# Node stage of a graph attention and mixture-of-experts layer: transposes between the halves of the products, and the bias added by an accumulating DMA

## The chip, the cores and the metric

The kernel runs on one core of a Trainium2 chip. The metric is the device time of one execution in microseconds. The kernel before took 2589.26 us in the median of 3 runs (2583.23 to 2590.76). A change within about 0.3% cannot be told from none.

## The reference

The layer is a graph attention step over 3125 nodes and 50,000 edges, followed by a mixture of eight experts. Cut to what the change touches:

```python
x = x + relu(gat(layernorm(x)) + bias)      # gat: softmax-weighted sum over the edges of each node and its own row
xn = layernorm(x)                           # eps 1e-5
proj = xn @ Wp.T                            # only its length is needed
gate = (proj / |proj|) @ l2norm(sim).T / temperature       # 8 scores per node, top 2
x = x + experts(xn)                         # needs xn of every node
```

The kernel never forms `proj`. With the Gram matrix G = Wp.T Wp (built earlier, held as two fp16 parts, upper triangle doubled) the squared length is xn . (G xn), and the scores come from xn times a premultiplied 1024x8 matrix `Msim`.

## The kernel before

The program is a row of blocks of code, each with one instruction list per engine, written by hand: the order in each list is the order of execution, and semaphores with counted waits order the engines. No planner takes part. The stages are projection, edge tables, softmax maxima, edge gathering with products, the node stage, slot assignment and the experts.

The change is in the node stage (L1043 to L1230). It handles the 3125 nodes in 25 blocks of 125 rows; every tile is 125 partitions by 1024 columns, and `p = i % 2` picks one of two buffers. For block i:

- SP loads two tiles of 500 KB: `own` (the node's own projected row) and `xt` (the input row), L1078 and L1079. It waits until `x2` of block i-2 is done.
- ACT scales `own` by the weight of the self loop, four instructions on L1187 (`scale_own`). It waits for both loads.
- DVE runs `layer_out`: four instructions on L1128 (gathered sum times 1/z plus `own`), the bias add on L1130, and ReLU plus `xt` on L1131, which ends block i's `x2`. `moments` (L1137 to L1140) gives mean and variance.
- ACT takes the root (L1194); DVE finishes the reciprocal in five tiny instructions (`inverse_std`, L1146 to L1150); ACT writes the normed rows twice, as fp32 `xn` (L1200) and as the fp16 high part (L1201); DVE's `low` (L1155) writes the fp16 low part.
- PE transposes both parts, 16 instructions (`turn_parts`, L1738); ACT copies them from PSUM to SBUF (`take_turned`, L1207).
- PE multiplies: first half of the triangle (12 matmuls, L1729), the scores (24 small matmuls, L1720), second half (24 matmuls, L1729). DVE's `length_and_scores` (L1160, L1162) reads the result.
- POOL stores `x2` to `out` (L1086) and the two fp16 parts to `x2n_d` (L1088), 500 KB each.

DVE's order in turn i is `inverse_std(i)`, `layer_out(i+1)`, `low(i)`, `moments(i+1)`, `length_and_scores(i-1)`. ACT's is `normed(i)`, `scale_own(i+2)`, `take_turned(i)`. PE's is transposes of block i, first half, scores, second half. POOL's is store of `x2` of block i, then store of the parts of block i. The bias is loaded once, broadcast to 125 partitions (L1073), and DVE waits for it on L1117.

Of the kernel before, what the change touches and what calls it, by code (L numbers as in the profile page):

```python
# [42 lines left out]
ROWS = 125  # L43
# [110 lines left out]
def program(nc, x, src, dst, W, att_src, att_dst, bias, Wp, sim, temp, W1, b1, W2, b2, out):  # L154
# [25 lines left out]
    with ctx:  # L180
# [43 lines left out]
        simT = sbuf(load_ctx, "simT", [P, 2, KD, NX], F16)  # L224
        s_st16, s_stw = sem("ed_st16"), sem("ed_stw")
        s_row = [sem(f"ed_row{p}") for p in range(2)]
        s_out = [sem(f"pj_out{p}") for p in range(2)]
        LATE = BLOCKS - 3
        with ExitStack() as c:
# [54 lines left out]
            with nc.Block() as block:  # L284
                @block.sync
                def _(sp):
                    def load(i):
                        if i >= 2:
                            sp.wait_ge(s_xf, i - 1)
                        sp.dma_start(xt[:, i % 2, :], rows_of(x, i)).then_inc(s_x[i % 2], 16)  # L290
                    load(0)
                    for n in range(4):
                        sp.dma_start(W_f[:, 2 * n:2 * n + 2, :],
                                     W[2 * n * P:(2 * n + 2) * P, :].rearrange("(k p) n -> p k n", p=P)).then_inc(s_ldw[n], 16)
                    load(1)
                    for n, a in enumerate((att_src, att_dst)):
                        sp.dma_start(att_b[:, n, :], a.rearrange("h c -> (h c)").partition_broadcast(ROWS)).then_inc(s_att, 16)
                    for i in range(2, BLOCKS):
                        load(i)
                        if i == 3:  # L300
                            sp.wait_ge(s_wlo, KD)
                            sp.dma_start(Wp_f[:, 1:KD + 1, :], Wp.rearrange("(k p) d -> p k d", p=P)).then_inc(s_ldp, 16)
                        if i == 15:

                            sp.wait_ge(s_rowv, 1)
                            sp.dma_start(lo_d.rearrange("(p r) n -> p (r n)", r=4), rowV[:, 0, :]).then_inc(s_vstore, 16)
                            sp.dma_start(dloc_d.rearrange("(p r) n -> p (r n)", r=4), rowV[:, 1, :]).then_inc(s_vstore, 16)
                    sp.wait_ge(s_vstore, 32)
                    sp.wait_ge(s_tr_ix, 3)
                    for t, d, n in ((stage_lo, lo_d, P), (stage_dl, dloc_d, ROWS)):  # L310
                        sp.dma_start(t, d[0:CHUNK, :].partition_broadcast(n)).then_inc(s_row[0], 16)
                    st_rows = st_d.rearrange("(b r) h -> r b h", r=ROWS)
                    for n, bs in enumerate((slice(0, LATE), slice(LATE, BLOCKS))):
                        sp.wait_ge(s_st16, 2 * n + 2)
                        sp.dma_start(st_rows[:, bs, :], st16[:, bs, :]).then_inc(s_stw, 16)

# [299 lines left out]
        with ExitStack() as c:  # L616
# [11 lines left out]
            w_ps, m_ps = v_all[:, 0:FIRST, :], v_all[:, 3, 0:KD * NX].rearrange("p (k e) -> p k e", e=NX)  # L628
            s_tab, s_zero = sem("ed_tab"), sem("ed_zero")
            s_gr, s_ghi, s_glo, s_m = sem("gr_mm"), sem("gr_hi"), sem("gr_lo"), sem("gr_msim")  # L630
# [28 lines left out]
            with nc.Block() as block:  # L659
                @block.sync  # L660
                def _(sp):
# [6 lines left out]
                    def tables():  # L668

                        sp.wait_ge(s_stw, 32)  # L670
                        sp.wait_ge(s_zero, 1)
# [72 lines left out]
                def _(pe):  # L744
# [3 lines left out]
                    for n in range(FIRST):  # L748
                        gram_piece(pe, n, w_ps[:, n, :])
                    pe.wait_ge(s_tab, 32)  # L750

# [291 lines left out]
        with edge_ctx, acc_ctx:  # L1043
            with ExitStack() as c:
                xt = sbuf(c, "n_xt", [ROWS, 2, D])
                own = sbuf(c, "n_own", [ROWS, 2, D])
                x2 = sbuf(c, "n_x2", [ROWS, 2, D])
                xn = sbuf(c, "n_xn", [ROWS, 2, D])
                bias_b = sbuf(c, "n_bias", [ROWS, D])
# [11 lines left out]
                sc_ps = psum(c, "n_sc", [P, 2, 512])  # L1061
                s_b, s_ch, s_d, s_e = sem("nd_bias"), sem("nd_chain"), sem("nd_d"), sem("nd_e")
                s_x = [sem(f"nd_x{p}") for p in range(2)]
                s_own, s_x2c, s_x2, s_ln, s_var, s_std = sem("nd_own"), sem("nd_x2c"), sem("nd_x2"), sem("nd_ln"), sem("nd_var"), sem("nd_std")
                s_rstd, s_xh = sem("nd_rstd"), sem("nd_xh")
# [4 lines left out]
                with nc.Block() as block:  # L1070
                    @block.sync
                    def _(sp):
                        sp.dma_start(bias_b[:, :], bias.partition_broadcast(ROWS)).then_inc(s_b, 16)  # L1073
                        for i in range(BLOCKS):
# [6 lines left out]
                    @block.gpsimd  # L1081
                    def _(pool):
                        for i in range(BLOCKS):
                            p = i % 2
                            pool.wait_ge(s_x2, i + 1)
                            pool.dma_start(rows_of(out, i), x2[:, p, :]).then_inc(s_out[p], 16)  # L1086
                            pool.wait_ge(s_xn, i + 1)
                            pool.dma_start(rows_of(x2n_d, i), xs[:, p, :, :].rearrange("r n d -> r (n d)")).then_inc(s_xo[p], 16)  # L1088
                        for p in range(2):
                            pool.wait_ge(s_out[p], 16 * ((BLOCKS + 1 - p) // 2))  # L1090
                            pool.wait_ge(s_xo[p], 16 * ((BLOCKS + 1 - p) // 2))

                    @block.vector
                    def _(dve):
# [21 lines left out]
                        dve.tensor_tensor(w_own, wk[:, 0, :, :], z_inv, ALU.mult).then_inc(s_d, 1)  # L1116
                        dve.wait_ge(s_b, 16)  # L1117

                        def layer_out(i):

                            p = i % 2
                            near = Chain(dve, s_x2c, 2 * i)
                            dve.wait_ge(s_own, i + 1)
                            if i >= 2:
                                dve.wait_ge(s_out[p], 16 * (i // 2))
                            for h in range(HEADS):
                                sl = slice(h * C, (h + 1) * C)
                                ins = dve.scalar_tensor_tensor(x2[:, p, sl], acc[:, i, sl], z_inv[:, i, h:h + 1], own[:, p, sl], ALU.mult, ALU.add)  # L1128
                            near(ins)
                            near(dve.tensor_tensor(own[:, p, :], x2[:, p, :], bias_b[:, :], ALU.add))  # L1130
                            dve.scalar_tensor_tensor(x2[:, p, :], own[:, p, :], 0.0, xt[:, p, :], ALU.max, ALU.add).then_inc(s_x2, 1)  # L1131
# [20 lines left out]
                        def low(i):  # L1152
                            p = i % 2
                            dve.wait_ge(s_xh, i + 1)
                            dve.tensor_tensor(xs[:, p, 1, :], xn[:, p, :], xs[:, p, 0, :], ALU.subtract).then_inc(s_xn, 1)  # L1155

                        def length_and_scores(i):
                            p = i % 2
                            dve.wait_ge(s_mm, i + 1)
                            dve.scalar_tensor_tensor(pj_ps[0:ROWS, p, :], pj_ps[0:ROWS, p, :], 1.0 / WS, xn[:, p, :], ALU.mult, ALU.mult,  # L1160
                                                     accum_out=nsq[:, i:i + 1])
# [4 lines left out]
                        for i in range(BLOCKS):  # L1166
# [4 lines left out]
                            if i + 1 < BLOCKS:  # L1171
                                moments(i + 1)
                            if i >= 1:
                                length_and_scores(i - 1)
                        length_and_scores(BLOCKS - 1)

                    @block.scalar
                    def _(act):
# [4 lines left out]
                        def scale_own(i):  # L1183
                            p = i % 2
                            act.wait_ge(s_x[p], 32 * (i // 2 + 1))
                            for h in range(HEADS):
# [3 lines left out]
                        def normed(i):  # L1190
# [3 lines left out]
                            act.activation(ln[:, p, 3:4], ln[:, p, 2:3], ACT.Sqrt).then_inc(s_std, 1)  # L1194
                            act.wait_ge(s_rstd, i + 1)
                            if i >= 2:
                                act.wait_ge(s_sc, i - 1)
                                act.wait_ge(s_tr, i - 1)
                                act.wait_ge(s_xo[p], 16 * (i // 2))
                            act.activation(xn[:, p, :], x2[:, p, :], ACT.Identity, bias=ln[:, p, 8:9], scale=ln[:, p, 7:8])  # L1200
                            act.activation(xs[:, p, 0, :], x2[:, p, :], ACT.Identity, bias=ln[:, p, 8:9], scale=ln[:, p, 7:8]).then_inc(s_xh, 1)  # L1201
# [15 lines left out]
                    def _(pe):  # L1217
                        for i in range(BLOCKS):
                            p = i % 2
                            pe.wait_ge(s_xn, i + 1)  # L1220
                            if i >= 1:
                                pe.wait_ge(s_xnT, i)
                            turn_parts(pe, tr_ps, xs[:, p, :, :], ident16).then_inc(s_tr, 1)
                            pe.wait_ge(s_xnT, i + 1)
# [3 lines left out]
                            triangle(pe, pj_ps[0:ROWS, p, :], lhs, gram, 0, range(KD // 2))  # L1228
                            product(pe, sc_ps[0:ROWS, p, 0:NX], lhs, Msim[:, :, :, :], range(KD), KD)
                            triangle(pe, pj_ps[0:ROWS, p, :], lhs, gram, 1, range(KD)).then_inc(s_mm, 1)  # L1230

# [555 lines left out]
```

## Time and profile before

| | |
|---|---|
| profiled execution, own time | 2587.55 us |
| its span in the trace | 2585.8 us |
| runs | median 2589.26 us, 2583.23 to 2590.76 |
| busy over the span | PE 80%, DVE 59%, ACT 43%, POOL 28% |
| granted TensorE clock, mean over the span | 0.892 |
| node stage in the trace | about 1456 to 1794 us |

The trace lists the instructions of each engine with start, duration and what ended the idle time before them. SPq and POOL rows of DMA instructions are the time of issue, not of the transfer; the landing is given apart. PEclk 1.00 is 2.4 GHz and 0.50 is 1.2 GHz. A DMA share of 1.00 would be all 16 DMA engines busy.

### The profile page before, as it was taken

Reading aid. Unit: us, or ns where it says so; the run is one execution under the profiler, and the core shown is the slowest. Engines: PE = TensorE matmul, PEld = TensorE weight load, DVE = VectorE, ACT = ScalarE, POOL = GpSimd, SP = SyncE. Lnnn points to the kernel's source line nnn. Section 1 sums busy time; section 2 is a strip of 40 time slices with the busy share of each in tenths; the row PEclk is TensorE's granted clock in tenths of the full one; section 3 lists DMA queues with packets and bytes.
Section 4 is the critical chain, followed back from the end, with each engine's and each line's share of the span. In section 5 each row is a group of like instructions: output and inputs, shape, how many; then the busy total and the mean of one; then the engine's idle time right before and its main releaser. Section 6 shows DMA issues by size and latency. Waiting matters only on the chain. (4 is left out here: it accounts for less than half of the span.)

```text
span 2585.8 us, 53583 instructions
## 1 busy us (share of the span) xinstructions
PE 2069.9 (80%) x14842; PEld 1476.4 (57%) x14843; DVE 1520.5 (59%) x4456; ACT 1117.3 (43%) x2399; POOL 716.5 (28%) x933
## 2 busy tenths in 40 slices
PE   2888987666678888888888478786498999898997
PEld 1555554444378788887888466664244444454553
DVE  3776764777766666666666576875744334434333
ACT  2333441111156676766667454542344334434332
POOL 0001000000055555555555200000223233333332
PEclk9899997555799999999999787988699999999999
DMA  4433343331078988988898544444545555564542
GB/s 137 154 110 113 118 150 94 122 133 59 1 252 299 310 300 297 309 299 296 289 305 299 183 173 168 172 162 148 205 138 198 207 176 200 199 213 159 174 159 89
DMA packets 141057, 489.14 MB, mean 189 GB/s; under 512 B 22449, under 2 KB 22659, under 8 KB 138829
## 3 DMA queue, kind: packets, MB, share of 16 engines
q0 software_dynamic: 98912, 346.99, 40.3%
q1 hardware_dynamic: 41853, 140.70, 14.9%
q8 instruction: 48, 0.79, 0.1%
q10 hardware_dynamic: 216, 0.43, 0.0%
q14 instruction: 28, 0.23, 0.0%
HBM read 418.06 MB, written 81.27 MB: 193 GB/s over the span
## 5 line engine op out<-in xcount | busy, mean ns | idle before, releaser
L1018 PE MATMUL main_ps<-rows,O 128*125 128x256 f16 x4992 | 614.0, 281 | 117.3 <-DVE acc L959 52.9
L1018 PEld LDWEIGHTS main_ps<-rows,O 128*125 128x125 f16 x4992 | 553.4, 141 | 139.0 <-issue 76.0
L1004 ACT ACTIVATE O<-O,pk 128x125 f16<-128x125 f16 x1664 | 499.5, 388 | 231.0 <-DVE O L974 196.8
L945 POOL DMA_INDIRECT rows<-projected,idx x416 | 396.1, 952 | 306.5 <-PE small_ps L1023 190.7
L978 DVE TENSOR_SCALAR O<-O,pk 128x125 f16<-128x125 f16 x1664 | 320.7, 278 | 14.8
L1720 PE MATMUL pj_ps<-gram,xsT 128*125 128x512 f16 x1200 | 291.8, 403 | 45.8 <-ACT xsT L382 44.6
L1671 PE MATMUL x_h<-w_p,gram 128*128 x1344 | 309.7, 388 | 13.8 <-ACT gram L1624 8.8
L1686 PE MATMUL x_o<-w_p,gram 128*128 x1344 | 312.5, 383 | 1.4 <-ACT gram L1640 1.4
L1720 PEld LDWEIGHTS pj_ps<-gram,xsT 128*125 128x125 f16 x1200 | 169.9, 145 | 155.9 <-ACT xsT L382 52.8
L1729 PE MATMUL n_pj<-gram,PK 128*125 128x512 f16 (+3 forms) x900 | 184.6, 367 | 55.5 <-ACT PK L1207 55.5
L1671 PEld LDWEIGHTS x_h<-w_p,gram 128*128 128x128 f16 x1344 | 132.2, 100 | 168.2 <-issue 29.4
L1686 PEld LDWEIGHTS x_o<-w_p,gram 128*128 128x128 f16 x1344 | 130.6, 99 | 150.3 <-issue 7.2
L974 DVE TENSOR_SCALAR O<-iota,pk 128x125 f16<-128x125 f16 x416 | 113.9, 274 | 142.7 <-PE small_ps L1023 101.3
L1729 PEld LDWEIGHTS n_pj<-gram,PK 128*125 128x125 f16 x900 | 126.6, 155 | 111.5 <-ACT PK L1207 59.9
L1632 ACT ACTIVATE h_g<-h_b 128x512 f32<-128x512 f32 x56 | 35.3, 630 | 290.0 <-DVE h_b L1604 290.0
L1594 DVE SCALAR_TENSOR_TENSOR x_o<-x_o,b_t 128x1024 f32<-128x1024 f32 x56 | 68.9, 1231 | 146.7 <-PE x_o L1686 146.7
L1570 POOL DMA_INDIRECT out_dram<-x_y,xi x56 | 76.6, 1367 | 235.4 <-DVE x_y L1597 235.4
L1624 ACT ACTIVATE gram<-x_tr 128x2048 f16<-128x2048 f16 x56 | 104.9, 1873 | 83.7 <-PE x_tr L1738 83.7
L1597 DVE SCALAR_TENSOR_TENSOR x_y<-x_o,gate_of_slot,x_y 128x1024 f32<-128x1024 f32 x56 | 71.9, 1283 | 100.6 <-DMA x_y<-out_dram,xi 98.7
L940 POOL COPY idx<-srcT 128x4 int32 (+1 forms) x104 | 20.5, 197 | 314.7 <-SPq L932 314.2
L740 ACT ACTIVATE d_p<-d_ps 128x64 f32 (+1 forms) x104 | 23.2, 223 | 188.2 <-PE d_ps L767 188.2
L1604 DVE SCALAR_TENSOR_TENSOR h_b<-x_h,b_b 128x512 f32<-128x512 f32 x56 | 38.6, 690 | 111.3 <-PE x_h L1671 102.3
(325 smaller groups left out, 2622.4 us busy)
## 6 DMA issues: line engine op xcount, KB each, us to landing
w_f<-in_L_ffn_W_dram SPq DMA_DIRECT2D x14, 2048.0 KB
b_t<-in_L_ffn_b_dram SPq DMA_DIRECT2D x56, 512.0 KB
xt<-in_x_dram SPq DMA_DIRECT2D x25, 500.0 KB
projected_f<-xp_f POOLq DMA_DIRECT2D x25, 500.0 KB, 3.7
projected<-xp POOLq DMA_DIRECT2D x25, 500.0 KB, 4.8
n_own<-projected_f SPq DMA_DIRECT2D x25, 500.0 KB
n_xt<-in_x_dram SPq DMA_DIRECT2D x25, 500.0 KB
out_dram<-n_x POOLq DMA_DIRECT2D x25, 500.0 KB, 9.9
```

The lines of the kernel that those rows point to most:

```text
L945: pool.indirect_dma_start(out=rows[:, 4 * p + k, :, :].rearrange("k n d -> k (n d)"), out_offset=None, in_=xp_d[:, :], in_offset=bass.Indi ...
L974: dve.tensor_scalar(O[:, k, 0, 0:ROWS], iota16[:, 0:ROWS], pk[:, p, k, 0:1], None, ALU.is_equal).then_inc(s_oh, 1)
L978: ins = dve.tensor_scalar(O[:, k, 1 + h, 0:ROWS], O[:, k, 0, 0:ROWS], pk[:, p, k, 1 + h:2 + h], None, ALU.mult)
L1004: ins = act.activation(O[:, k, 1 + HEADS + h, 0:ROWS], O[:, k, 0, 0:ROWS], ACT.Copy, scale=pk[:, p, k, w:w + 1])
L1018: pe.matmul(main_ps[0:ROWS, h * C:(h + 1) * C], O[:, k, 1 + HEADS * a + h, 0:ROWS], rows[:, 4 * p + k, b, h * C:(h + 1) * C], start=first ...
L1570: pool.indirect_dma_start(out=out[:, :], out_offset=bass.IndirectOffsetOnAxis(ap=xi[:, 2 + p, :], axis=0), in_=y[:, p, :], in_offset=None, ...
L1597: dve.scalar_tensor_tensor(y[:, p, :], o_ps[:, p, :], at1(gateT, i), y[:, p, :], ALU.mult, ALU.add).then_inc(s_eo, 1)
L1624: act.activation(xgT[:, p, :, :, :], tr_ps[:, :, :, :], ACT.Copy).then_inc(s_xT, 1)
L1671: ins = pe.matmul(h_ps[:, :], xgT[:, p, a, k, :], w, start=(k == 0 and a == b), stop=(k == KD - 1 and a == 1))
L1686: ins = pe.matmul(o_ps[:, p, n * 512:(n + 1) * 512], hT[:, p, a, f, :], w, start=(f == 0 and a == b), stop=(f == KF - 1 and a == 1))
L1720: ins = pe.matmul(out, lhs[:, a, k, :], rhs[:, b, k, :], start=(k == 0 and a == b), stop=(k == last - 1 and a == 1))
L1729: ins = pe.matmul(out[:, cols], lhs[:, a, k, :], rhs[:, b, k, cols], start=(k == 0 and a == b), stop=True, skip_group_check=True)
```

## The change

Four edits in the node stage, and a merging of semaphores elsewhere.

1. The 16 transposes of block i+1 are issued between the scores and the second half of block i. Only block 0's stand ahead of the loop.
2. `xn` gets a third buffer; `length_and_scores(i-2)` instead of (i-1) stands at the end of DVE's turn i, and ACT's wait for it is one block looser.
3. The bias add leaves DVE. After `scale_own(i)`, POOL issues a DMA from `bias_b` to `own` in SBUF that adds (`add_bias`). The first two stand ahead of POOL's loop, the one for block i+2 after the two stores of its turn i. DVE's `layer_out` waits for that DMA, and writes the sum to `own` instead of `x2`.
4. The wait for the bias load moves from DVE to the first `scale_own`.
5. `s_stw` and `s_tab` of the edge tables become one semaphore, with the wait raised from 32 to 64.

```diff
-                xn = sbuf(c, "n_xn", [ROWS, 2, D])
+                xn = sbuf(c, "n_xn", [ROWS, 3, D])
...
+                        def add_bias(i):
+
+                            p = i % 2
+                            pool.wait_ge(s_own, i + 1)
+                            pool.dma_start(own[:, p, :], bias_b[:, :], accum_op=ALU.add).then_inc(s_ob[p], 16)
+                        add_bias(0)
+                        add_bias(1)
                         for i in range(BLOCKS):
                             p = i % 2
                             pool.wait_ge(s_x2, i + 1)
                             pool.dma_start(rows_of(out, i), x2[:, p, :]).then_inc(s_out[p], 16)
                             pool.wait_ge(s_xn, i + 1)
                             pool.dma_start(rows_of(x2n_d, i), xs[:, p, :, :].rearrange("r n d -> r (n d)")).then_inc(s_xo[p], 16)
+                            if i + 2 < BLOCKS:
+                                add_bias(i + 2)
...
-                        dve.wait_ge(s_b, 16)
...
-                            near = Chain(dve, s_x2c, 2 * i)
-                            dve.wait_ge(s_own, i + 1)
+                            dve.wait_ge(s_ob[p], 16 * (i // 2 + 1))
...
-                                ins = dve.scalar_tensor_tensor(x2[:, p, sl], acc[:, i, sl], z_inv[:, i, h:h + 1], own[:, p, sl], ALU.mult, ALU.add)
-                            near(ins)
-                            near(dve.tensor_tensor(own[:, p, :], x2[:, p, :], bias_b[:, :], ALU.add))
+                                ins = dve.scalar_tensor_tensor(own[:, p, sl], acc[:, i, sl], z_inv[:, i, h:h + 1], own[:, p, sl], ALU.mult, ALU.add)
+                            ins.then_inc(s_x2c, 1)
+                            dve.wait_ge(s_x2c, i + 1)
...
-                            if i >= 1:
-                                length_and_scores(i - 1)
-                        length_and_scores(BLOCKS - 1)
+                            if i >= 2:
+                                length_and_scores(i - 2)
+                        for i in (BLOCKS - 2, BLOCKS - 1):
+                            length_and_scores(i)
...
-                            act.wait_ge(s_x[p], 32 * (i // 2 + 1))
+                            act.wait_ge(s_x[p], 32 * (i // 2 + 1) + (16 if p == 0 else 0))
...
+                            if i >= 3:
+                                act.wait_ge(s_sc, i - 2)
                             if i >= 2:
-                                act.wait_ge(s_sc, i - 1)
...
-                        for i in range(BLOCKS):
-                            p = i % 2
+                        def turn(i):
                             pe.wait_ge(s_xn, i + 1)
                             if i >= 1:
                                 pe.wait_ge(s_xnT, i)
-                            turn_parts(pe, tr_ps, xs[:, p, :, :], ident16).then_inc(s_tr, 1)
+                            turn_parts(pe, tr_ps, xs[:, i % 2, :, :], ident16).then_inc(s_tr, 1)
+                        turn(0)
+                        for i in range(BLOCKS):
+                            p = i % 2
                             pe.wait_ge(s_xnT, i + 1)
...
                             product(pe, sc_ps[0:ROWS, p, 0:NX], lhs, Msim[:, :, :, :], range(KD), KD)
+                            if i + 1 < BLOCKS:
+                                turn(i + 1)
                             triangle(pe, pj_ps[0:ROWS, p, :], lhs, gram, 1, range(KD)).then_inc(s_mm, 1)
```

## Rows read from the trace of the kernel before

**Rows 1.** Span; timeline at both ends of the stage (start us, us, engine).

```profile
span 2585.8 us, 53583 instructions
...
1476.51 0.25 SPq L1078 DMA_DIRECT2D n_own<-projected_f  x1
...
1482.56 1.67 DVE L1128 SCALAR_TENSOR_TENSOR n_x<-acc,n_wk,n_own 125x256 f32<-125x256 f32 x4
...
1486.77 0.25 SPq L1078 DMA_DIRECT2D n_own<-projected_f  x1
...
1768.53 1.22 DVE L1131 SCALAR_TENSOR_TENSOR n_x<-n_own,n_xt 125x1024 f32<-125x1024 f32 x1
...
1794.12 0.26 SPq L1330 DMA_DIRECT2D tcol<-n_L_ffn_temperature_dram  x1
```

**Rows 2.** Timeline, one block at full clock; in brackets idle time before and its releaser.

```profile
1625.06 1.04 PE L1738 MATMUL n_tr<-ident,PK 125*128 125x125 f16 x16
1626.14 1.84 ACT L1207 ACTIVATE PK<-n_tr 128x2000 f16<-128x2000 f16 x1 [1.97 <-PE n_tr L1738]
1628.03 1.85 PE L1729 MATMUL n_pj<-gram,PK 128*125 128x512 f16 x12 [1.93 <-ACT PK L1207]
1629.12 1.66 DVE L1128 SCALAR_TENSOR_TENSOR n_x<-acc,n_wk,n_own 125x256 f32<-125x256 f32 x4
...
1630.82 1.22 DVE L1130 TENSOR_TENSOR n_own<-n_x,n_bias 125x1024 f32<-125x1024 f32 x1
1631.08 4.42 PE L1729 MATMUL n_pj<-gram,PK 128*125 128x512 f16 x24
1632.07 1.23 DVE L1131 SCALAR_TENSOR_TENSOR n_x<-n_own,n_xt 125x1024 f32<-125x1024 f32 x1
...
1635.33 1.04 PE L1738 MATMUL n_tr<-ident,PK 125*128 125x125 f16 x16
```

**Rows 3.** Timeline, from the end of a block's x2 to its loads, stores and next scaling.

```profile
1608.27 1.22 DVE L1131 SCALAR_TENSOR_TENSOR n_x<-n_own,n_xt 125x1024 f32<-125x1024 f32 x1
1609.52 0.25 SPq L1078 DMA_DIRECT2D n_own<-projected_f  x1
1610.92 0.52 POOL L1088 DMA_DIRECT2D x_after_gnn_normed<-PK  x1 [12.49 <-DVE PK L1155]
1611.44 0.52 POOL L1086 DMA_DIRECT2D out_dram<-n_x  x1
1622.47 1.71 ACT L1187 ACTIVATE n_own<-n_own,n_wk 125x256 f32<-125x256 f32 x4 [1.13 <-DMA n_xt<-in_x_dram]
```

**Rows 4.** Waits between the second and the last block: total us, times, longest.

```profile
ACT n_own L1187 <- DMA n_xt<-in_x_dram: 66.8, 21, 4.5
PE n_pj L1729 <- ACT PK L1207: 51.7, 23, 3.3
```

**Rows 5.** Timeline, the first two scalings, each released by its loads.

```profile
1470.46 1.70 ACT L1187 ACTIVATE n_own<-n_own,n_wk 125x256 f32<-125x256 f32 x4 [10.08 <-DMA n_xt<-in_x_dram]
1478.29 1.70 ACT L1187 ACTIVATE n_own<-n_own,n_wk 125x256 f32<-125x256 f32 x4 [6.12 <-DMA n_xt<-in_x_dram]
```

**Rows 6.** Windows: us, busy us of five engines, clock, DMA share, GB/s.

```profile
1465.00:1475.00 10.00, 0.00 (x0) 0.00 (x0) 2.67 (x5) 1.70 (x4) 0.00 (x0) 0.50 0.32 131
1612.00:1616.00 4.00, 3.83 (x33) 2.83 (x32) 1.23 (x3) 0.13 (x1) 0.00 (x0) 0.95 0.90 286
1616.00:1620.00 4.00, 2.24 (x23) 1.93 (x23) 2.33 (x11) 2.83 (x3) 0.00 (x0) 1.00 0.33 135
```

**Rows 7.** Issue to landing: stores of x2 (all; the first), stores of parts (all).

```profile
DMA to landing us min/median/max: 5.0/9.9/10.5
...
DMA to landing us min/median/max: 7.8/7.8/7.8
...
DMA to landing us min/median/max: 3.6/7.7/8.2
```

**Rows 8.** Window of a stretch at half clock, columns as above.

```profile
1605.50:1612.40 6.90, 6.90 (x40) 5.33 (x39) 6.62 (x11) 4.01 (x6) 1.04 (x2) 0.51 0.28 92
```

More of the change, by code:

```diff
@@ L224, in program @@
         simT = sbuf(load_ctx, "simT", [P, 2, KD, NX], F16)
-        s_st16, s_stw = sem("ed_st16"), sem("ed_stw")
+        s_st16, s_tab = sem("ed_st16"), sem("ed_tab")
         s_row = [sem(f"ed_row{p}") for p in range(2)]
@@ L314, in _ @@
                         sp.wait_ge(s_st16, 2 * n + 2)
-                        sp.dma_start(st_rows[:, bs, :], st16[:, bs, :]).then_inc(s_stw, 16)
+                        sp.dma_start(st_rows[:, bs, :], st16[:, bs, :]).then_inc(s_tab, 16)
                 @block.gpsimd
@@ L628, in program @@
             w_ps, m_ps = v_all[:, 0:FIRST, :], v_all[:, 3, 0:KD * NX].rearrange("p (k e) -> p k e", e=NX)
-            s_tab, s_zero = sem("ed_tab"), sem("ed_zero")
+            s_zero = sem("ed_zero")
             s_gr, s_ghi, s_glo, s_m = sem("gr_mm"), sem("gr_hi"), sem("gr_lo"), sem("gr_msim")
@@ L668, in tables @@
                     def tables():
-                        sp.wait_ge(s_stw, 32)
+                        sp.wait_ge(s_tab, 32)
                         sp.wait_ge(s_zero, 1)
@@ L749, in _ @@
                         gram_piece(pe, n, w_ps[:, n, :])
-                    pe.wait_ge(s_tab, 32)
+                    pe.wait_ge(s_tab, 64)
                     def body(i, j, p):
@@ L1061, in program @@
                 sc_ps = psum(c, "n_sc", [P, 2, 512])
-                s_b, s_ch, s_d, s_e = sem("nd_bias"), sem("nd_chain"), sem("nd_d"), sem("nd_e")
+                s_ch, s_d, s_e = sem("nd_chain"), sem("nd_d"), sem("nd_e")
                 s_x = [sem(f"nd_x{p}") for p in range(2)]
+                s_ob = [sem(f"nd_own_bias{p}") for p in range(2)]
                 s_own, s_x2c, s_x2, s_ln, s_var, s_std = sem("nd_own"), sem("nd_x2c"), sem("nd_x2"), sem("nd_ln"), sem("nd_var"), sem("nd_std")
@@ L1072, in _ @@
                     def _(sp):
-                        sp.dma_start(bias_b[:, :], bias.partition_broadcast(ROWS)).then_inc(s_b, 16)
+                        sp.dma_start(bias_b[:, :], bias.partition_broadcast(ROWS)).then_inc(s_x[0], 16)
                         for i in range(BLOCKS):
@@ L1154, in low @@
                             dve.wait_ge(s_xh, i + 1)
-                            dve.tensor_tensor(xs[:, p, 1, :], xn[:, p, :], xs[:, p, 0, :], ALU.subtract).then_inc(s_xn, 1)
+                            dve.tensor_tensor(xs[:, p, 1, :], xn[:, i % 3, :], xs[:, p, 0, :], ALU.subtract).then_inc(s_xn, 1)
                         def length_and_scores(i):
@@ L1159, in length_and_scores @@
                             dve.wait_ge(s_mm, i + 1)
-                            dve.scalar_tensor_tensor(pj_ps[0:ROWS, p, :], pj_ps[0:ROWS, p, :], 1.0 / WS, xn[:, p, :], ALU.mult, ALU.mult,
+                            dve.scalar_tensor_tensor(pj_ps[0:ROWS, p, :], pj_ps[0:ROWS, p, :], 1.0 / WS, xn[:, i % 3, :], ALU.mult, ALU.mult,
                                                      accum_out=nsq[:, i:i + 1])
@@ L1195, in normed @@
                             act.wait_ge(s_rstd, i + 1)
+                            if i >= 3:
+                                act.wait_ge(s_sc, i - 2)
                             if i >= 2:
-                                act.wait_ge(s_sc, i - 1)
                                 act.wait_ge(s_tr, i - 1)
                                 act.wait_ge(s_xo[p], 16 * (i // 2))
-                            act.activation(xn[:, p, :], x2[:, p, :], ACT.Identity, bias=ln[:, p, 8:9], scale=ln[:, p, 7:8])
+                            act.activation(xn[:, i % 3, :], x2[:, p, :], ACT.Identity, bias=ln[:, p, 8:9], scale=ln[:, p, 7:8])
                             act.activation(xs[:, p, 0, :], x2[:, p, :], ACT.Identity, bias=ln[:, p, 8:9], scale=ln[:, p, 7:8]).then_inc(s_xh, 1)
```

## The prediction

> **What bounds the kernel now.** I read four views, in this order. The page's slices and the timeline first place the stage. Call X(i) the end of L1131 for block i, when `x2` of that block is done. SP issues the loads for block i+2 0.03 us later, so X(0) is 1476.48, X(1) is 1486.74, X(24) is 1769.75, and the next stage starts at 1794.1 [rows 1]. The mean period is (1769.75 - 1486.74)/23 = 12.30 us per block.
>
> The timeline of one block at 2.4 GHz gives the PE loop. Transposes start at 1625.06, the first half waits for ACT's copy and starts at 1628.03, and the next transposes start at 1635.33 [rows 2]. That is 10.27 us, of which 1.93 is the wait for the copy. The waits view has it 23 times, 51.7 us [rows 4]. Other blocks are longer because the clock is 1.2 GHz for part of them, with PE then busy without a gap [rows 8].
>
> The same view shows a second limit, nearly as close. ACT waits for the loads in 21 blocks of 23, 66.8 us [rows 4]. A load issued at 1609.52 releases the scaling at 1622.47, 12.95 us later [rows 3]. The 23 such pairs run from 12.6 to 14.2. The windows say why. With only SP's loads in flight the DMA share is 0.32, that is 0.32 x 16 = 5.1 engines, at 131 GB/s [rows 6]. The next pair of tiles takes 1478.29 - 1470.46 = 7.83 us [rows 5], so 25 rows of 4 KB per tile and engine at 0.157 us each. The Trainium skill ("DMA: Bandwidth & Descriptors", "Why a DMA increments its semaphore by 16 and not by 1") says that a transfer of this path uses the largest number of engines up to 16 that divides its slowest dimension, 5 for 125 rows, the lowest-numbered ones; the 5.1 agrees.
>
 A pair of loads and two stores keep them busy 7.83 + 2.5 = 10.3 us per block, as long as PE's own loop. The stores land late for it: those of the parts 7.7 us after issue in the median, those of `x2`, issued right behind, 9.9 us [rows 7].
>
> **The change, part by part.** *Transposes between the halves.* ACT's copy now has the second half (4.25 us, 1631.08 to 1635.33) to hide under [rows 2]. PE's loop falls from 10.27 to 1625.06-1626.10 plus 1628.03-1635.33 = 1.04 + 7.30 = 8.3 us at full clock. It pays only where nothing else is later.
>
> *Looser scores and the third `xn`.* No instruction is added. `length_and_scores(i-2)` comes after the second half of i-2, which now ends a block earlier relative to it, so I price its wait at 0. If that cover went, DVE would wait for at most one second half, 4.42 us, and the forecast below has more slack than that.
>
> *Bias add off DVE.* L1130 to L1131 starts is 1.25 us, so `layer_out` shrinks from 4.18 (1629.12 to 1633.30) to 2.93 us [rows 2].
>
> *The adding DMA.* This is the new price. The place decides it. In POOL's list the add for block i+2 stands behind the store of the parts of block i, which waits for `low(i)`, which DVE runs after `layer_out(i+1)`. So it cannot be issued before X(i+1). And `layer_out(i+2)` is the next long piece on DVE and waits for its landing. That closes a loop inside one period:
>
> X(i+1) to the issue of the parts is 1610.92 - 1609.49 = 1.43; the second DMA of the pair is issued 0.52 later, at 1.95 [rows 3]. The add takes the place that the store of `x2` has now. Its landing time, A, is in no row. Nearest is that store, same size, same queue, same neighbours: 9.9 us. Below, the same two stores with no load beside them land after 5.0, and a lone one after 3.6 [rows 7]; above, an add that moves twice the rows costs 8 more of them, each alternating with one of a load, 16 x 0.157 = 2.5 us, giving 12.4. I take 9.9, since X(i+1) also issues the next loads 1.4 us ahead, as now. Then 0.1 us to wake DVE (estimate) and 2.93: period = 1.95 + 9.9 + 0.1 + 2.93 = 14.9 us.
>
> A second loop runs over two periods. Loads slow from 12.95 to 12.95 + 1.25 = 14.2 us by the add's own rows, then scaling 1.71, POOL's start 0.3 (estimate from 0.29 between the end of `low` and the issue), A, 0.1, 2.93: (19.2 + A)/2 = 14.6 us. Less, but close. The five engines need 7.83 + 3 x 1.25 = 11.6. PE needs 8.3, and at most twice that, 16.7, in a block wholly at 1.2 GHz.
>
> *What is queued behind the wait.* While POOL waits for the scaling of block i+2, the store of `x2(i+1)` waits behind it. It is needed two periods later and costs 0. Behind DVE's wait stands everything: `low`, so the transposes, so PE's second half. That is in the period.
>
> *Prologue.* Scaling 0 ends at 1472.16 [rows 5]. The add follows at 1472.46 and lands after 7.8, the time of the first store beside loads [rows 7]; `layer_out(0)` ends at 1472.46 + 7.8 + 0.1 + 2.93 = 1483.3. DVE's second `layer_out` started 6.08 after X(0) [rows 1]; kept so, X(1) = 1483.3 + 6.1 + 2.9 = 1492.3, later by 5.5 us.
>
> *Tail.* After X(24), with the durations of [rows 2]: transposes of 23 from 1.3 (1.22 for `low`) to 2.3, second half of 22 to 6.6, first half and scores of 23 (1631.08 - 1628.03 = 3.05) to 9.7, transposes of 24 to 10.7, second half of 23 to 15.0, first half and scores of 24 to 18.0, its second half to 22.4, then 1.8 to the next stage: 24.2 us, against 1794.12 - 1769.75 = 24.4 now [rows 1]. That is -0.2.
>
> *Bias wait and merged semaphores.* The bias is ahead of the first loads in SP's queue, and the scaling waits for those anyway: 0. The table loads follow the table stores through SP's own wait, so 64 is reached when 32 was: 0.
>
> Sum: 5.5 + 23 x (14.9 - 12.3) - 0.2 = 5.5 + 59.8 - 0.2 = +65.1 us. The profiled execution took 2587.55 us, 1.7 below the median of the runs, so 2587.55 + 65.1 = 2652.7, in round numbers 2653 us. Every microsecond of A is worth 23 us.
>
> **Rivals.** *The add reads twice.* The add has to fetch both `own` and `bias_b`. If that doubles its rows, A = 12.4, period 17.4, 23 x 5.1 + 5.3 = +122: 2710 us. Nothing in the trace shows an adding DMA. The Trainium skill ("Collectives: The Full Stack", "The bandwidth ceiling: the fold count and why AG ≠ RS ≠ AR") says that an add in the DMA path needs two source reads, and that this halved a reduce-scatter's rate; no row here bears on it.
>
> *PE stays at 1.2 GHz.* With some 6 us of idle time per period, a slower PE would need 16.7 us: 23 x 4.4 + 5.3 = +107, 2694 us. For it: while PE idled before its first block the clock was 0.50 [rows 6]. Against: it is back at 0.95 to 1.00 a few microseconds after a stretch at 0.51, although PE waits in each block [rows 6, 8].
>
> *Less contention.* The add is SBUF to SBUF and may be on fewer or other engines than the loads. With A = 7.7, like the first store of a pair, and loads at 12.95: (18.0 + 7.7)/2 = 12.9, so 23 x 0.6 + 5 = +19: 2606 us. The DMA page of the Trainium skill, in the section named above, lets GpSimd's queue place a 125-row transfer either on 16 engines or on 5 consecutive ones that rotate; the second would give something like this.
>
> *The landing is as without loads.* A = 5.0: the one-period loop is 10.0, the other (19.2 + 5.0)/2 = 12.1. 23 x (-0.2) + 2.7 = -2: 2586 us, no change. The gain of PE is then hidden by the loads.
>
> *Faster.* The add runs wholly off the five engines of the loads and lands as the fastest store, A = 3.6: (18.0 + 3.6)/2 = 10.8, still above the 10.3 of those engines. 23 x (-1.5) + 1.3 = -33: 2554 us. It decides from A below about 5.3, where (19.2 + A)/2 passes 12.3. For it speaks that once the stores' first burst is over two thirds of the engines are idle, 1 - 0.33 [rows 6]. Against it speak the medians of 7.7 and 9.9 us of the stores that POOL issues now [rows 7].
>
> **How the numbers follow.** The forecast with A from 9.3 to 10.5 has 0.48. The double read has 0.13, the slow clock 0.07, less contention 0.15; these are all slower, 0.83. No change has 0.11 and faster 0.06. 0.3% is 7.8 us, which is also what a measurement can tell. The range from 2592 to 2712 us takes in all slower cases and leaves out no change and faster, 0.17, and a little above; the likeliest case by itself is 2639 to 2667.
>
> **What would show it.** Period 14.9 us between L1078 issues; DVE idle ahead of L1128, some 5 us per block, released by the add's landing near 9.9 us; PE idle ahead of the transposes, released by L1155; no wait of L1729 for L1207; five-engine share of DMA with longer loads, about 14 us. Wrong if DVE's wait for the add is below 1 us, if L1128 is released by ACT, or if the stage (1456 to 1794) becomes shorter than 338 us.

## The result and the profile after

The changed kernel takes 2692.88 us in the median (2690.13 to 2694.91, 4 runs) against 2586.24 for the kernel before (2579.61 to 2590.76, 4 runs). The ratio is 1.042, 95% interval 1.0396 to 1.0444: slower. That lies in the range given. The forecast was 2653, so the loss is 107 us where 65 were forecast.

Line numbers shift in the changed kernel: `scale_own` is L1196, the adding DMA L1088, `layer_out` L1136 and L1139, `low` L1163, the copy of the transposes L1217, the transposes L1752. First the ends of the stage in its timeline, which answer to [rows 1]:

```profile
span 2691.7 us, 53581 instructions
...
1460.59 0.26 SPq L1074 DMA_DIRECT2D n_bias<-in_L_gnn_bias_dram  x1
...
1488.36 0.25 SPq L1079 DMA_DIRECT2D n_own<-projected_f  x1
...
1498.26 0.25 SPq L1079 DMA_DIRECT2D n_own<-projected_f  x1
...
1874.70 1.22 DVE L1139 SCALAR_TENSOR_TENSOR n_x<-n_own,n_xt 125x1024 f32<-125x1024 f32 x1
...
1901.89 0.26 SPq L1344 DMA_DIRECT2D tcol<-n_L_ffn_temperature_dram  x1
```

The stage, from the load of the bias to the first load of the next stage, takes 1901.89 - 1460.59 = 441.3 us. Before it took 337.9, since the same load of the bias stood at 1456.20 and the next stage began at 1794.12 [rows 1]. So 103.4 of the 105.9 us between the two spans are in this stage; below, the length of the stage is always taken in this way. X(i) is, as in the prediction, the end of `layer_out` for block i. From X(1) = 1498.23 to X(24) = 1875.92 it is 377.7 us, 16.4 per block against 12.3.

One period in the timeline, which answers to [rows 2] and [rows 3]:

```profile
1618.24 1.22 DVE L1163 TENSOR_TENSOR PK<-n_xn,PK 125x1024 f16<-125x1024 f32 x1
1618.35 0.25 SPq L1079 DMA_DIRECT2D n_own<-projected_f  x1
...
1619.51 1.86 PE L1752 MATMUL n_tr<-ident,PK 125*128 125x125 f16 x16 [6.95 <-DVE PK L1163]
1619.75 0.53 POOL L1096 DMA_DIRECT2D x_after_gnn_normed<-PK  x1 [14.64 <-DVE PK L1163]
...
1620.27 0.89 POOL L1088 DMA_DIRECT2D n_own<-n_bias  x1
...
1620.82 0.88 POOL L1094 DMA_DIRECT2D out_dram<-n_x  x1
...
1631.68 1.67 DVE L1136 SCALAR_TENSOR_TENSOR n_own<-acc,n_wk,n_own 125x256 f32<-125x256 f32 x4 [7.21 <-DMA n_own<-n_bias]
1633.39 1.22 DVE L1139 SCALAR_TENSOR_TENSOR n_x<-n_own,n_xt 125x1024 f32<-125x1024 f32 x1
1634.01 1.71 ACT L1196 ACTIVATE n_own<-n_own,n_wk 125x256 f32<-125x256 f32 x4 [7.13 <-DMA n_xt<-in_x_dram]
1634.53 1.22 DVE L1163 TENSOR_TENSOR PK<-n_xn,PK 125x1024 f16<-125x1024 f32 x1
```

Read it from the first line. `low` ends, POOL issues the parts' store, then the add at 1620.27. DVE starts `layer_out` at 1631.68, 11.4 us later, having stood idle for 7.21 us until the add landed. L1139 ends at 1634.61, and the next turn begins. The load issued at 1618.35 is the one that releases the scaling at 1634.01: 15.7 us, where it was 12.95 in the block of [rows 3] and 13.2 in the median.

The waits between X(2) and X(23), us in total, times, longest, and below them the stage's DMAs with their median time to landing; these answer to [rows 4] and [rows 7]:

```profile
DVE n_own L1136 <- DMA n_own<-n_bias: 151.5, 21, 8.1
ACT n_own L1196 <- DMA n_xt<-in_x_dram: 150.5, 21, 7.6
...
PE n_tr L1752 <- DVE PK L1163: 126.9, 21, 7.5
...
n_own<-n_bias POOLq DMA_DIRECT2D x25, 500.0 KB, 11.3
out_dram<-n_x POOLq DMA_DIRECT2D x25, 500.0 KB, 13.1
x_after_gnn_normed<-PK POOLq DMA_DIRECT2D x25, 500.0 KB, 7.8
```

DVE, which had no such wait before, now waits 7.2 us in every block. PE's wait for ACT's copy is gone but for one, and in its place stands one of 6.0 us for `low`. The stores of `x2` now go out last and land after 13.1 us instead of 9.9.

### The profile page after: what moved, and what is told of

Read it like the earlier page. It is cut to its first block and busy times, and to the rows that moved or that the text cites. A ratio compares the mean times of both kernels' runs of the same rounds, so it can differ in the third digit from the quotient of the medians.

```text
span 2691.7 us, 53581 instructions
## 1 busy us (share of the span) xinstructions
PE 2076.4 (77%) x14842; PEld 1482.9 (55%) x14843; DVE 1493.0 (55%) x4431; ACT 1119.6 (42%) x2399; POOL 738.2 (27%) x958
## 5 line engine op out<-in xcount | busy, mean ns | idle before, releaser
L1734 PE MATMUL pj_ps<-gram,xsT 128*125 128x512 f16 x1200 | 284.3, 396 | 52.7 <-ACT xsT L382 52.4
L1752 PE MATMUL n_tr<-ident,PK 125*128 125x125 f16 x400 | 45.7, 306 | 176.2 <-DVE PK L1163 176.2
L1136 DVE SCALAR_TENSOR_TENSOR n_own<-acc,n_wk,n_own 125x256 f32<-125x256 f32 x100 | 41.8, 480 | 185.1 <-DMA n_own<-n_bias 185.1
L1752 PEld LDWEIGHTS n_tr<-ident,PK 125*128 125x128 f16 x400 | 39.4, 144 | 178.3 <-DVE PK L1163 178.3
## 6 DMA issues: line engine op xcount, KB each, us to landing
n_own<-n_bias POOLq DMA_DIRECT2D x25, 500.0 KB, 11.3
```

What stands on the lines that cost most here:

```text
L1734: ins = pe.matmul(out, lhs[:, a, k, :], rhs[:, b, k, :], start=(k == 0 and a == b), stop=(k == last - 1 and a == 1))
L1752: ins = pe.transpose(out[:, part, k, 0:n], parts[:, part, k * P:(k + 1) * P], ident16[0:n, 0:n])
```

## The experiments

The runs were made in four groups on more than one chip. The kernel before took 2586, 2481, 2597 and 2598 us in them; in the second group (add_only, turns_only, copy_not_add, split_loads) the stage begins 100 us earlier in the trace. So I compare the ratio to the kernel before of the same group, and the length of the stage, taken as above. The kernel before has a trace from the first group alone; for the other kernels, the difference of the stage to it agrees within 9 us with the difference of the medians inside their group. The periods are means from X(1) to X(24).

| kernel | ratio (95%) | stage, us | period, us |
|---|---|---|---|
| before | 1 | 337.9 | 12.3 |
| changed | 1.042 (1.0396 to 1.0444) | 441.3 | 16.4 |
| add_only | 1.0431 (1.0379 to 1.0483) | 445.7 | 16.4 |
| turns_only | 0.990 (0.9868 to 0.9932) | 311.0 | 11.2 |
| copy_not_add | 1.0329 (1.0276 to 1.0381) | 415.9 | 15.6 |
| split_loads | 1.0175 (1.0123 to 1.0228) | 379.7 | 14.1 |
| turns_split | 0.976 (0.9726 to 0.9793) | 271.2 | 9.7 |
| before_split | 0.9878 (0.9829 to 0.9927) | 303.8 | 11.0 |
| deep_add | 1.0119 (1.0086 to 1.0152) | 362.2 | 12.8 |
| deep_split | 0.9837 (0.9801 to 0.9873) | 288.4 | 10.1 |
| add_ahead_of_parts | 1.0333 (1.0316 to 1.035) | 420.7 | 15.6 |
| deep_split_order | 0.9771 (0.9751 to 0.9792) | 277.4 | 9.7 |
| pool_adds | 0.9635 (0.9613 to 0.9656) | 243.9 | 8.4 |

**One part at a time.** turns_only is the changed kernel with the bias back on DVE.

```diff
-                            dve.wait_ge(s_ob[p], 16 * (i // 2 + 1))
+                            dve.wait_ge(s_own, i + 1)
+                            near = Chain(dve, s_x2c, 2 * i)
...
+                            near(dve.tensor_tensor(own[:, p, :], x2[:, p, :], bias_b[:, :], ALU.add))
```

> The changed kernel with the bias add back on DVE (L1130 and its semaphore as before); the moved transposes, the third xn and the later length_and_scores stay. Theory (the adding DMA closes a loop inside one period, and alone makes the slowdown): the period is then the work of the five engines that loads and stores share, 10.3 us, or a little more where the clock is 1.2 GHz; 23 x (10.3..11 - 12.3) = -30..-46 us, so 2540 to 2558 us, faster than before. Rival (the transposes between the halves tie PE's second half to DVE's low and take part in the slowdown): slower than before, over 2595 us.

Measured: 2456.4 us against 2481.1 in that group, ratio 0.990, stage 311.0. The sign is that of the theory; the gain, 27 us of stage, is just under the 30 to 46 expected. It belongs to the moved transposes and the later `length_and_scores` together, which were not tried apart. Its waits say where the rest lies (from its second block to the last):

```profile
ACT n_own L1188 <- DMA n_xt<-in_x_dram: 94.6, 23, 5.2
...
PE n_tr L1744 <- DVE PK L1155: 75.1, 21, 33.4
DVE n_ln L1146 <- ACT n_ln L1195: 48.2, 23, 4.2
```

ACT's list has the scaling of i+2 ahead of the copy of i. With a shorter period the load is later for it, 4.1 us per block, and the copy and the root stand behind. So DVE waits 2.1 us per block for the root (1.7 before); with the loads cut, in turns_split below, this wait falls to 0.6.

add_only is the other half: the adding DMA with PE's and DVE's old order.

```diff
-                        def turn(i):
+                        for i in range(BLOCKS):
+                            p = i % 2
                             pe.wait_ge(s_xn, i + 1)
...
-                        turn(0)
-                        for i in range(BLOCKS):
-                            p = i % 2
...
-                            if i + 1 < BLOCKS:
-                                turn(i + 1)
```

> The kernel before with only the adding DMA and its waits (third xn kept, PE's transposes and length_and_scores in the old order). Theory: period 16.2 us as in the changed kernel, 2685 to 2700 us, since PE is not in the loop. Rival (the two edits share the loss): clearly under 2680 us.

Measured: ratio 1.0431, stage 445.7, period 16.4, landing of the add 11.3 us. The absolute figure in the expectation was for the first group; the stage and the ratio are those of the changed kernel, to the 9 us named above. The whole loss is the adding DMA's, and the moved transposes bring next to nothing beside it.

**Is it the adding?** copy_not_add has a plain copy in the same place, which leaves the node's own row out.

```diff
-                            pool.dma_start(own[:, p, :], bias_b[:, :], accum_op=ALU.add).then_inc(s_ob[p], 16)
+                            pool.dma_start(own[:, p, :], bias_b[:, :]).then_inc(s_ob[p], 16)
```

> The changed kernel with a plain copy from bias_b to own in place of the adding one, so the node's own row is left out of the sum and the bias stays; same size, queue, place and waits. Theory A (the adding costs more than a copy, as each row is fetched twice): landing falls from 11.3 to about 9.9 us as for the second store before, period 14.9, 2693 - 23 x 1.3 = about 2660 us. Rival (any transfer in this place is as late, or SBUF to SBUF is itself slow): landing 11.3, 2693 us.

Measured: landing 10.6 us, ratio 1.0329, stage 415.9. That is between the theory and its rival. The DMA view tells more: packets, MB and share of 16 engines of POOL's queue over the blocks. First before (23 blocks, 283.0 us), then changed (21 blocks, 342.3 us), then copy_not_add (21 blocks, 326.4 us):

```profile
q0 software_dynamic: 6624, 23.56, 25.0%
```

```profile
q0 software_dynamic: 9072, 32.26, 38.4%
```

```profile
q0 software_dynamic: 9072, 32.26, 30.3%
```

Per block that is 0.250 x 16 x 283.0 / 23 = 49.2 engine-us for two stores, 0.384 x 16 x 342.3 / 21 = 100.1 with the add, and 0.303 x 16 x 326.4 / 21 = 75.4 with the copy. So a store is 24.6, the copy adds 26.2, and the add 50.9: the adding transfer has as many packets as the copy and occupies the engines 1.95 times as long. The Trainium skill ("Collectives: The Full Stack", "The bandwidth ceiling: the fold count and why AG ≠ RS ≠ AR") says that such an add needs two source reads; the 1.95 agrees with this. But the landing is only 0.7 us of 11.3 longer for it, and half of that lies in the issue, from whose start the landing is counted: 0.90 us in the median, 0.52 for the copy.

**Is it the five engines?** split_loads is the changed kernel with each load in two pieces, of 120 and 5 rows.

```diff
-                            sp.dma_start(own[:, p, :], rows_of(own_d, i)).then_inc(s_x[p], 16)
-                            sp.dma_start(xt[:, p, :], rows_of(x, i)).then_inc(s_x[p], 16)
+                            for to, t in ((own, own_d), (xt, x)):
+                                for lo, hi in ((0, 120), (120, ROWS)):
+                                    sp.dma_start(to[lo:hi, p, :], rows_of(t, i)[lo:hi, :]).then_inc(s_x[p], 16)
```

> The changed kernel with each 125-row load of own and xt cut into rows 0 to 120 and 120 to 125. Theory (the add is late because its rows stand behind the loads' on five shared engines): the loads spread over 15 engines, DMA share with loads alone rises from 0.32 to over 0.7, landing of the add falls to about 8 us, period 5.0 + 8 = 13, 23 x (-3.3) = about 2617 us. Rival (the landing is the add's own time): landing near 11 us, time 2685 or more.

Measured: landing 9.2 us, period 14.1, ratio 1.0175, stage 379.7. The window with SP's loads alone, as [rows 6] had it with a share of 0.32:

```profile
1360.00:1366.00 6.00, 0.00 (x0) 0.00 (x0) 0.07 (x1) 0.00 (x0) 0.00 (x0) 0.50 0.86 208
```

The loads do now spread over the engines (0.86, 208 GB/s for 131). The landing falls by 2.1 us, not by the 3.3 expected, and the stage by 62 us. In all four kernels with the DMA in this place the formula of the prediction holds, with the landing that each had: 4.98 + 11.3 = 16.3, + 10.6 = 15.6, + 9.2 = 14.2. The means in the table are 16.4, 15.6 and 14.1; from X(2) on, without the irregular start, they are 16.2, 15.3 and 14.1.

before_split has the same cut in the kernel before.

> The kernel before with only the loads cut in rows 0 to 120 and 120 to 125. Theory (PE's loop of 10.27 us with its wait for the copy, 13.5 in blocks at 1.2 GHz, is the bound of before, the loads are second): only blocks at 11 to 12 us can shrink; period 12.3 -> 11.7 to 12.3, stage 338 -> 324 to 338 us. Rival (the loads were the first bound): period under 11.3, stage under 316 us.

Measured: ratio 0.9878, stage 303.8. The rival was right. The windows of the two, over blocks 1 to 24, show it; before first:

```profile
1486.80:1769.80 283.00, 230.20 (x1735) 178.22 (x1736) 204.63 (x435) 137.09 (x184) 23.86 (x46) 0.84 0.47 165
```

```profile
1501.90:1755.80 253.90, 208.43 (x1735) 162.91 (x1736) 204.09 (x435) 135.80 (x184) 23.85 (x46) 0.92 0.60 183
```

PE has the same work in both, but the granted clock is 0.84 in the one and 0.92 in the other. The period is 13.5 us in five of the last 22 blocks of before_split and 10.3 in most others, while before has eight of 13.5, two of 15.2 and only about five of 10.3. The four runs of before_split have a mean clock of 0.893 to 0.900 over the whole kernel, the seven of the kernel before in that group 0.888 to 0.894, so it is not one profile's doing. So the late loads cost not only waits but, with them, stretches at 1.2 GHz. Why the clock falls less often when the loads are early was not settled.

turns_split is turns_only with the same cut.

> The kernel turns_only (transposes moved, bias add on DVE) with each 125-row load cut into rows 0 to 120 and 120 to 125. turns_only had period 11.2 us and ACT waiting 94.6 us for loads. Theory (what is left there is the five engines of the loads): load lands some 9 us after issue, the period falls to DVE's 9.2 us of work plus its 1.1 us wait for the root, 10.0 to 10.3; stage (bias load to the next stage's first load) 311 -> 285 to 291 us. Rival (PE's clock or the wait chain through ACT sets it): stage stays within 4 us of 311.

Measured: ratio 0.976, stage 271.2, period 9.7. All engines over 222.4 us:

```profile
1498.10:1720.50 222.40, 200.06 (x1708) 157.39 (x1709) 202.27 (x432) 136.01 (x184) 23.84 (x46) 0.92 0.69 208
```

DVE is busy 202.3 of 222.4 us, 8.8 us per block, and waits 0.6 us per block for the root. PE is busy nearly as long, 200.1 us, but part of that at half clock; at full clock it needs 8.3 of the 9.7. I read DVE as the bound; that pool_adds below, with 1.25 us less on DVE, has a period of 8.2 speaks for it.

**Is it the place?** add_ahead_of_parts puts the add ahead of the parts' store in POOL's list, so that it no longer waits for `low(i)`.

```diff
+                            if i + 2 < BLOCKS:
+                                add_bias(i + 2)
                             pool.wait_ge(s_xn, i + 1)
                             pool.dma_start(rows_of(x2n_d, i), xs[:, p, :, :].rearrange("r n d -> r (n d)")).then_inc(s_xo[p], 16)
-                            if i + 2 < BLOCKS:
-                                add_bias(i + 2)
```

> The changed kernel with POOL's list in the order store of x2(i), adding DMA for i+2, store of the parts of i. Theory (the add's place behind the parts' store closes the one-period loop): the add no longer waits for low(i); what binds is the two-period loop, (load 14 to 15.8 + 5.0 + landing 8 to 10)/2 = 13.5 to 15.4 against 16.4, stage 441 -> 375 to 420 us. Rival (the order on POOL does not matter, the landing does): period 16.2, stage near 441.

Measured: ratio 1.0333, stage 420.7. Landing of the add 8.4 us. The ends of `layer_out` now alternate, some 10 and some 20 us apart, a mean of 15.6: the one-period loop is open, and the loop over two periods binds. Two periods take 29.1 to 32.2 us, 30.8 in the mean. It gains only 21 us, because there the load, the scaling and the add stand in a row: 17.3 + 1.7 + 0.3 + 8.4 + 3.0 = 30.7 us, with the load now 17.3 us in the median.

deep_add opens both loops: three buffers of `own` and `xt`, loads, scaling and add one block earlier. On ACT the scaling moves behind the copy of the transposes.

```diff
-                xt = sbuf(c, "n_xt", [ROWS, 2, D])
-                own = sbuf(c, "n_own", [ROWS, 2, D])
+                xt = sbuf(c, "n_xt", [ROWS, 3, D])
+                own = sbuf(c, "n_own", [ROWS, 3, D])
...
-                            if i >= 2:
-                                sp.wait_ge(s_x2, i - 1)
+                            if i >= 3:
+                                sp.wait_ge(s_x2, i - 2)
...
-                            if i + 2 < BLOCKS:
-                                add_bias(i + 2)
+                            if i + 3 < BLOCKS:
+                                add_bias(i + 3)
...
-                            if i + 2 < BLOCKS:
-                                scale_own(i + 2)
                             take_turned(i)
+                            if i + 3 < BLOCKS:
+                                scale_own(i + 3)
```

> The changed kernel with three buffers of own and xt: loads, scaling and the adding DMA one block earlier (DVE has two periods until it needs the add), scaling behind take_turned on ACT. Loads not cut. Theory (the add costs by its landing inside a one-period loop; once the loop is open what is left is the work of the five shared engines, 7.83 for loads + 2.5 for stores + 2.5 to 3.3 for the add): period 12.8 to 13.6, stage 441 -> 355 to 375 us, so still slower than before. Rival (the add delays DVE or PE in another way): period stays near 16.

Measured: ratio 1.0119, stage 362.2, periods of 12.8 and 13.4 in turn for most of the stage. No wait of DVE for the add is left in its list of waits, and the stage is 79 us shorter than the changed kernel's, so most of the loss was the loop; 24 us of it stay. Other waits have taken its place (17 blocks):

```profile
DVE n_ln L1156 <- ACT n_ln L1205: 87.6, 17, 6.9
...
ACT n_own L1198 <- DMA n_xt<-in_x_dram: 41.0, 16, 3.5
```

The period fits the work of the five shared engines, as the theory had it. It also fits a chain through ACT: the root waits behind the scaling, which waits for a load issued 20.3 us earlier, and DVE stands idle 5.2 us per block for the root. This run does not tell the two apart.

deep_split cuts the loads as well.

> deep_add with the loads cut in rows 0 to 120 and 120 to 125. Theory: both limits gone; all 16 engines have some 8.7 us of rows per block, PE 8.3, DVE 7.9 plus a wait of 1.1: period 9 to 10, stage 265 to 285 us, less than turns_split if DVE was its bound. Rival (an adding DMA is never worth it: its engine time, twice a copy's, delays loads and stores): stage longer than in turns_split.

Measured: ratio 0.9837, stage 288.4; not below turns_split's 271.2, so the rival was right on that. A window of it:

```profile
1525.00:1735.00 210.00, 185.98 (x1588) 147.14 (x1587) 161.34 (x377) 121.14 (x163) 40.85 (x64) 0.92 0.96 249
```

The DMA share is 0.96: all 16 engines are nearly always busy. But DVE also waited 2.2 us per block for the root behind the scaling, so deep_split_order puts ACT's old order back.

```diff
-                            take_turned(i)
                             if i + 3 < BLOCKS:
                                 scale_own(i + 3)
+                            take_turned(i)
```

> deep_split (period 10.2 us, DMA share 0.96) with ACT's scaling of block i+3 ahead of take_turned(i) again, so that the root does not stand behind it. Theory (all 16 DMA engines are the bound once loads are spread and the add is there): period 9.7 to 10.2, stage 278 to 288 us, still over turns_split's 271. Rival (ACT's order was the bound: DVE waited 2.2 us per block for the root): period 8.4 to 9.0, stage under 262 us.

Measured: ratio 0.9771, stage 277.4. ACT's order was worth 11 us by the stage and 17 by the ratios, and the rest stayed. Its window and what is left of its waits:

```profile
1540.00:1740.00 200.00, 185.79 (x1603) 147.07 (x1602) 156.47 (x364) 119.56 (x155) 37.35 (x59) 0.93 0.91 248
```

```profile
ACT n_own L1199 <- DMA n_xt<-in_x_dram: 33.7, 12, 6.5
DVE n_ln L1157 <- ACT n_ln L1206: 29.4, 20, 5.3
```

DVE has 156 us of work in 200, and the DMA share is 0.91, or 8.8 us of every period of 9.7. Half of the scalings still wait for their loads, although these are now spread (0.86 with the loads alone, in split_loads), and DVE waits for the root behind them. That the engines of the transfers are the bound is read from this and from pool_adds; no run shows it by itself.

**The version the experiments point to.** pool_adds takes the bias off DVE, but adds it with an instruction of POOL in the same place, with the loads cut.

```diff
-                            pool.dma_start(own[:, p, :], bias_b[:, :], accum_op=ALU.add).then_inc(s_ob[p], 16)
+                            pool.tensor_tensor(own[:, p, :], own[:, p, :], bias_b[:, :], ALU.add).then_inc(s_ob[p], 1)
```

> The changed kernel with loads cut in two and the bias added by a GpSimd tensor_tensor on own in the place of the adding DMA (the add is an instruction of POOL, no transfer). Theory (what was wrong with the move off DVE is the DMA, not the move): POOL's add of 125x1024 takes some 1.5 to 3 us, DVE sheds 1.25 of 9.7 us: period 8.4 to 9.2, stage 245 to 262 us, ratio about 0.97 or lower, the fastest. Rival (VectorE and GpSimd get in each other's way on SBUF): DVE's instructions lengthen by as much as they lose, stage 271 us or more.

Measured: 2504.31 us (2500.04 to 2508.79) against 2598.05, ratio 0.9635, stage 243.9: faster than both kernels. Against turns_split, which has the bias on DVE, the stage is 27 us shorter. One turn of it:

```profile
1602.38 1.22 DVE L1164 TENSOR_TENSOR PK<-n_xn,PK 125x1024 f16<-125x1024 f32 x1
...
1603.65 1.05 PE L1753 MATMUL n_tr<-ident,PK 125*128 125x125 f16 x16
...
1604.11 0.68 DVE L1147 BATCH_NORM_STATS2 n_stat<-n_x 125x6 f32<-125x512 f32 x1
1604.43 2.37 POOL L1089 TENSOR_TENSOR n_own<-n_own,n_bias 125x1024 f32<-125x1024 f32 x1
...
1605.14 1.22 DVE L1169 SCALAR_TENSOR_TENSOR n_pj<-n_pj,n_xn 125x1024 f32<-125x1024 f32 x1
...
1607.72 1.67 DVE L1137 SCALAR_TENSOR_TENSOR n_own<-acc,n_wk,n_own 125x256 f32<-125x256 f32 x4
...
1610.57 1.22 DVE L1164 TENSOR_TENSOR PK<-n_xn,PK 125x1024 f16<-125x1024 f32 x1
```

The add takes 2.37 us in place of 11.3 and is done before DVE asks for it, so L1137 has no wait. The period is 8.19 us from X(5) on, which is PE's 8.3 of the prediction at full clock, and now the moved transposes pay in full. With the loads not cut this version was not run.

## Why the prediction came out as it did

The forecast named the right term and sized it too low. 2693 us lies outside the 2639 to 2667 of its likeliest case; the range holds it because its rivals stretched it to 2712. That the slow-clock rival had 2694 is a coincidence: what it described was not in the loop, as its item below shows.

- *The loop inside one period.* Right. The add is issued 1.95 us after X(i+1), DVE stands idle until it lands, and `layer_out` ends 2.95 to 2.96 us after the landing in all 25 blocks. With A = 11.3 the formula gives 16.3, measured 16.2 to 16.4 in most blocks.
- *A, the landing of the add.* This is the term that failed, 9.9 against 11.3. At 23 us per microsecond it is 32 us, most of the 38 by which the stage was under-forecast (103.4 against 65.1). 0.7 of the 1.4 us is the adding (copy_not_add lands after 10.6), 0.4 of it the longer issue. The other 0.7 is there with a plain copy too; whether it is the SBUF source or the third transfer in the queue was not tried.
- *Prologue and first periods.* X(1) came 7.1 us later relative to the load of the bias, 5.5 forecast. The second period took 22.1 us, because X(0) to X(2) obeys the loop over two periods, 32.0 us. I had let the one-period loop run from the start: another 6 us, of which the last period, 13.2 us, gave back 3.
- *Tail.* 26.0 us against 24.2.
- *Loads.* 15.7 us in the median, for 14.2. With the plain copy they take 15.0, so the adding accounts for 0.7 of the 1.5 us; the rest is not explained. The 12.95 that the forecast started from was low, too: the median before is 13.2.
- *The rival of the double read.* Right on engine time, 1.95 times; too high on the landing, 12.4 for 11.3.
- *PE stays at 1.2 GHz.* The granted clock of blocks 3 to 23 is 0.76, for 0.84 before, and transposes after the long wait run at half clock (1.86 us for 1.04). It costs nothing there: what ends every block's `layer_out` is the landing, 2.96 us earlier, whatever PE does, and DVE's idle 7.2 us end with the add.
- *Less contention, the landing as without loads, faster.* They needed landings of 7.7, 5.0 and 3.6 us. None of the 25 adds landed before 8.2.
- *Transposes between the halves.* Right that they pay only where nothing else is later: nothing beside the add, 27 us without it, and together with early loads and a cheap add the full 8.2 us period.
- *What bounds the kernel before.* Wrong in its weighting. I held PE's loop to be first and the loads second; cutting the loads alone took 34 us from the stage.
- *Other edits.* Nothing in the traces speaks against pricing the moved wait for the bias and the merged semaphores at 0; neither was tried alone. The later `length_and_scores` leaves DVE no wait for the products; the kernel before had 12 of them, 33.0 us together. The forecast gave nothing for that, and beside the add it brings nothing.

## What to carry to other kernels

A DMA in place of a 1.2 us vector instruction is costly above all where somebody needs it within one period: find the instruction that it must follow and the one that waits for it, and add its landing beside the other traffic, 11.3 us here, not its issue. Opening the loop took most of the loss away but made no gain: with three buffers and cut loads the stage took 277.4 us (deep_split_order), with the bias left on DVE 271.2 (turns_split). Before adding a transfer, read how many DMA engines the ones beside it use; 125 rows gave five, and two pieces of 120 and 5 rows took 34 to 74 us from this stage (before and deep_add). If another compute engine is idle, an instruction there (2.37 us on POOL) may do the same work with no queue in its way.

## What the runs showed that was not expected

- An adding DMA of 500 KB occupies the DMA engines 50.9 engine-us, a plain copy of the same bytes in its place 26.2.
- POOL's 2.37 us add ran beside DVE's `bn_stats` and `length_and_scores`, and these kept their durations: 0.68 us for L1147 and 1.22 for L1169, as the same instructions had before, 0.67 and 1.23. The contention that the rival supposed did not show.
- Early loads raised the granted clock of the same PE work from 0.84 to 0.92; why is open.
